# Two edge aggregations of a graph network: waits taken once in four pairs, four gathers on one semaphore

## The reference

```
x = x + _L0_gnn_ref(_layernorm(x), src, dst, edge_weight, W, b)      # layer 1
    msgs = features[edge_src] * edge_weight[:, None]
    agg  = segment_sum(msgs, edge_dst, num_segments=12500)
    out  = einsum('ni,oi->no', agg, W) + b
x = x + _L1_gnn_ref(_layernorm(x), stack([src, dst]), edge_weight, ...) # layer 3
    h = x @ W;  gathered = A_values[:, None] * h[col]
    agg = segment_sum(gathered, row, num_segments=12500)             # then batch norm, relu
```

## Time and profile before

| | before |
|---|---|
| time, median of 3 runs | 8190.22 us |
| span of the profiled execution | 8556.1 us |
| first aggregation, first to last gather | 211.7 to 2484.6 us |
| second aggregation, first to last gather | 4122.7 to 6425.6 us |
| gathers in each / matmul pairs in each | 1563 / 1664 |
| adds of VectorE, both | 3328, 422 ns each |

### The profile page before, as it was taken

One profiled execution on the slowest core, in us unless ns is written; L12 is line 12 of the kernel. 1 busy time (PEld: TensorE's weight loads), 2 busy tenths in 40 slices (PEclk: granted clock), 3 DMA queues, 4 the chain that ended last, 5 costly groups with the idle time before them and its releaser, 6 DMA issues. The chain is left out here.

```text
span 8556.1 us, 91570 instructions
## 1 busy us (share of the span) xinstructions
PE 5764.1 (67%) x19687; PEld 3851.9 (45%) x19687; DVE 4500.6 (53%) x8804; ACT 3777.5 (44%) x9645; POOL 5818.2 (68%) x7545
## 2 busy tenths in 40 slices
PE   5454555555556999968465656565556888888866
PEld 4333333333335666644243434443333555555545
DVE  5354555545456999958454454554457222222227
ACT  5555555655554222226355555555555222222213
POOL 3666666666644222226688888888886688888875
PEclk8677767676665999989666767766678999999988
DMA  7333333333332111126333333333333322222218
GB/s 227 91 90 89 90 91 91 92 91 91 91 116 81 45 50 49 46 65 206 99 90 91 91 89 91 88 91 90 88 91 129 95 59 57 56 58 55 56 47 324
DMA packets 498681, 797.56 MB, mean 93 GB/s; under 512 B 121278, under 2 KB 363563, under 8 KB 498059
## 3 DMA queue, kind: packets, MB, share of 16 engines
q0 software_dynamic: 200256, 453.47, 19.5%
q1 hardware_dynamic: 297904, 338.22, 12.2%
HBM read 595.60 MB, written 197.30 MB: 93 GB/s over the span
## 5 line engine op out<-in xcount | busy, mean ns | idle before, releaser
L1013 PE MATMUL part<-rows,spread 128*128 x6656 | 2481.5, 527 | 1990.5 <-issue 984.0
L1013 PEld LDWEIGHTS part<-rows,spread 128*128 128x128 f32 x6656 | 1613.8, 261 | 2797.6 <-issue 2539.6
L970 DVE TENSOR_TENSOR agg<-agg,part 128x257 f32 (+1 forms) x3328 | 1405.1, 422 | 2230.5 <-PE part L1013 721.7
L953 POOL DMA_INDIRECT rows<-f,row x1563 | 1549.6, 991 | 733.8 <-issue 453.0
L1037 ACT ACTIVATE spread<-iota,place 128x128 f32<-128x128 f32 x3328 | 1016.1, 387 | 2038.2 <-PE part L1013 1309.5
L953 POOL DMA_INDIRECT rows<-h,row x1563 | 1550.5, 992 | 258.4 <-issue 256.3
L1952 POOL DMA_INDIRECT rows<-gat,src x1122 | 1077.9, 961 | 185.0 <-issue 185.0
L1043 ACT ACTIVATE spread<-spread,weight 128x128 f32<-128x128 f32 x3328 | 1017.5, 388 | 14.1 <-ACT spread L1039 0.3
L2030 PE MATMUL y_ps<-agg,hid 128*128 128x256 f32 x3136 | 765.4, 405 | 190.7 <-DVE y_all L2160 190.7
L2030 PEld LDWEIGHTS y_ps<-agg,hid 128*128 128x128 f32 x3136 | 640.9, 206 | 342.2 <-DVE y_all L2160 209.5
L404 POOL COPY spare<-pay 128x1024 f32<-128x1024 f32 x105 | 222.3, 2117 | 735.7 <-DVE pay L391 505.7
(11 more groups left out here) (400 smaller groups left out, 6449.2 us busy)
## 6 DMA issues: line engine op xcount, KB each, us to landing
expert_rows<-y_all SPq DMA_DIRECT2D x196, 256.0 KB
made<-expert_rows SPq DMA_DIRECT2D x49, 1024.0 KB
x<-x SPq DMA_DIRECT2D x42, 896.0 KB
rows<-f,row POOLq DMA_INDIRECT x1563
rows<-h,row POOLq DMA_INDIRECT x1563
rows<-gat,src POOLq DMA_INDIRECT x1122
xbuf<-zero SPq DMA_DIRECT2D x16, 1024.0 KB
x<-xbuf SPq DMA_DIRECT2D x32, 512.0 KB
```

The costliest lines, as they stand in the source:

```text
L953: pool.indirect_dma_start(out=rows[:, u, 0:D], out_offset=None, in_=table, in_offset=bass.IndirectOffsetOnAxis(ap=q.row[:, i:i + 1], axis= ...
L970: nc.vector.tensor_tensor(sum_t, sum_t, part[:, p % NB, 0:WIDE], ALU.add).then_inc(added, 1)
L1013: nc.tensor.matmul(part[:, p % NB, 0:WIDE], spread[:, p % (2 * BANKS), :], row_p, start=True, stop=True).then_inc(multiplied, 1)
```

## The change

It changes who waits how often in `aggregate_edges`; no instruction that computes or moves data is added, removed or reordered. `HAND` is 4.

- The 32 slots share 8 semaphores, four gathers each; SyncE waits for four gathers with one wait and adds four to `landed`: 391 instructions at line 932 for 1563.
- VectorE waits for `multiplied` once in four pairs, for all four; its wait for its own add before stays for every pair.
- TensorE waits for `spread_done` and for free banks once in four pairs, for all four.

```
-        gathered = [s.sem(f"gathered{u}") for u in range(SPAN)]
+        gathered = [s.sem(f"gathered{u}") for u in range(SPAN // HAND)]
...
-                    for i in range(j * BANKS, (j + 1) * BANKS):
+                    for i in range(j * BANKS, (j + 1) * BANKS, HAND):
                         if i < FILLED:
-                            sp.wait_ge(gathered[i % SPAN], i // SPAN * 16 + 16)
-                        sp.sem_inc(landed, 1)
+                            sp.wait_ge(gathered[i % SPAN // HAND], (i // SPAN * HAND + min(HAND, FILLED - i)) * 16)
+                        sp.sem_inc(landed, HAND)
...
-                                            in_offset=bass.IndirectOffsetOnAxis(ap=q.row[:, i:i + 1], axis=0)).then_inc(gathered[u], 16)
+                                            in_offset=bass.IndirectOffsetOnAxis(ap=q.row[:, i:i + 1], axis=0)).then_inc(gathered[u // HAND], 16)
...
                         if u % 4 == 0:
                             tiles = load_tiles(nc, dve, q, p, regs)
-                        dve.wait_ge(multiplied, p + 1)
-
+                            dve.wait_ge(multiplied, p + 4)
                         if p:
                             dve.wait_ge(added, p)
...
-                    pe.wait_ge(spread_done, p + 1)
-                    if p >= NB:
-                        pe.wait_ge(added, p - NB + 1)
+                    if p % 4 == 0:
+                        pe.wait_ge(spread_done, p + 4)
+                        if p + 4 > NB:
+                            pe.wait_ge(added, p + 4 - NB)
```

More of the change, by code:

```diff
@@ L21 @@
 HALF = LANES // 2
-BANKS, RING = 8, 4
+BANKS, RING, HAND = 8, 4, 4
 FILLED = -(-EDGES // P)
```

## The result

| | before | after |
|---|---|---|
| time, median | 8191.28 us (8185.34 to 8197.51, 18 runs) | 8206.51 us (8193.91 to 8228.15, 18 runs) |
| ratio to before | | 1.0020, 95% interval 1.0013 to 1.0026 |
| span of the profiled execution | 8556.1 us | 8203.1 us |

The change makes the kernel 15 us slower. That is little, but the interval of the ratio does not reach 1; 8140 us was forecast. The profiled span, on the other hand, fell by 353 us, to the median. The two do not fit, and the first question is which of the two profiles speaks for the kernel. The profile on which the forecast rests was of a disturbed execution; one further profile would have shown it. From here on, "before" is compared by the first of these new profiles.

What follows compares the result with a forecast made beforehand. GpSimd's gathers were taken to bound both aggregations, with stops at the ring to be won. From the median 8190 us, -44 (stops) and -5 (adds) gave 8141, say 8140 us; the overall range was 8030 to 8210 us.

Steps and rivals of the forecast that it cites:

- What bounds the kernel now: Both aggregations: GpSimd's gathers are the bound, 4576 us, and its 342 us of stops can be won.
- stops at the ring: GpSimd's waits for SyncE's `freed` at line 926 in both aggregations: 342 us profiled, 75 us taken for an ordinary execution.
- rows 4 to 7: Profile rows on SyncE's waits for TensorE, 1109.9 us, adds 0.63 or 2.80 us apart, and long sequencer instructions.
- The part that removes instructions: DVE, PE and SP: 6.7 to 4.5 sequencer instructions a pair, winning 202 us of stops in the profiled execution.
- 59% fewer stops: In slow stretches the chain loses 0.63 us a pair instead of 1.55, so ring stops shrink by about that share.
- What of it is there in an ordinary execution: Both aggregations: unprofiled ring stops are bounded, not known; 75 us taken, gain 44 us, bounds 0 and 202.
- the 44 us of gain: Both aggregations: 59% of the 75 us of ring stops taken for an ordinary execution.
- The first case: If all 366 us are lost in the two aggregations, 83 us are above GpSimd's pace and stops are zero.
- The first rival: Both aggregations: recording makes the slow stretches, GpSimd paces without a stop; no change, 8185 us; chance 0.30.
- The adds themselves: VectorE: three in four adds lose 0.07 us, counting only behind the last gathers, 5 us for both aggregations.
- The other parts: SyncE's shared semaphores, TensorE's matrix and bank waits: up to 3.8 us of lag once, or 0.9 us a group.
- The second rival: Second aggregation, seven banks: TensorE's blocks delay VectorE 1.4 us a group; slower, 8240 us; chance 0.13.

Runs made afterwards that it cites:

- these new profiles: The kernel before, unchanged, profiled twice more: spans 8194.3 and 8190.8 us.
- padded: The changed kernel with each removed wait put back as one already fulfilled: median 8224.22 us, 1.0031 of before.
- step4: The kernel before, each gather keeping its own semaphore, but SyncE counting landed in steps of four: 1.0007 of before.
- pe_dve: The change without SyncE's part, against before: TensorE and VectorE hand over blocks of four, chunks counted one by one: 1.0011 of before.
- before_again: The kernel before, unchanged, profiled again: span 8194.3 us.
- fine_norest_all: Before with TensorE's and VectorE's blocks, pair-by-pair waits in the last 32 pairs, no memsets between second-aggregation and attention gathers: 7768.72 us, 0.9491 of before.

## Why the prediction was wrong

- *What bounds the kernel now.* "GpSimd is the bound" held. "Its stops at the ring are what can be won" did not: in three later profiles of the two kernels there are none. The reading of rows 4 to 7 was a true reading of a disturbed execution. What the chain did in that one execution was taken for what it always does.
- *The part that removes instructions.* 6.7 to 4.5 instructions a pair was right in kind (84,238 for 91,570 in the whole trace), the 59% fewer stops had nothing to act on. The profiled span did fall, by 353 us where 207 were forecast, but not because of the change: unchanged, it fell as far.
- *What of it is there in an ordinary execution.* This is the step that failed. Three values were open for the stops at the ring, 0, 146 and 342 us; 75 us was taken and the measured one is 0, so the 44 us of gain had nothing to come from. The first case had the stops right, but not for its reason, that all 366 us are lost in the aggregations (449 - 366 = 83 us above GpSimd's pace). Before, profiled again, has 83 + 64 = 147 us above the pace, nearly all of them slow gathers: of the 362 us between the two profiles 302 lie between first and last gathers and 34 in the tails. The first rival had the span fall for a reason of its own (the recording), and `padded` and the two profiles of before speak against that reason; its conclusion, that GpSimd paces both aggregations without a stop, is what the runs show.
- *The adds themselves.* 0.07 us off each add was taken: four adds take 2.11 us after, (2.11 - 0.42) / 3 = 0.563 us from one to the next, for 0.63 before, and 0.63 again in `padded`, which has the wait back. The size was right, the place was not. The 60 and 30 adds behind the last gathers were counted from the disturbed profile; before, profiled again, has 16 and 15, worth 31 x 0.75 x 0.07 = 1.6 us instead of 5. And these were not won, since VectorE waits there for TensorE's block. The rule of the Trainium skill ("VectorE: DVE Perf Modes", The DRAIN you can't avoid), that leaving out semaphores between vector operations gains nothing, would have left the adds 0.63 us apart, and that is not what these rows show. The two cases are not alike, though: the wait for the add before stayed here, and what went is a wait instruction of its own that stood between.
- *The other parts.* "Up to 3.8 us of lag, once" was the price of SyncE's steps if their cover was gone. The cover (SyncE waits for TensorE) was gone: it was part of the disturbed execution, and TensorE really waits for SyncE 388 times. The price was met once in each aggregation, +4.8 and +3.3 us (`step4`), and it was not in the sum. Neither was any price for TensorE and VectorE handing over blocks to each other, 9 us (`pe_dve`): this part had looked at each engine's wait by itself.
- *The second rival* had the mechanism and the sign. It expected VectorE to reach its fifth add 3.9 us after the first at the low clock level; 4.59 us were measured. It placed the loss in all groups and took seven banks for its cause, which gave 94 us. Between the gathers it is hidden, and in the tails it shows with eight banks too: 3.5 us there and 5.5 us with seven (`pe_dve`).
- Sum as measured, by the tails: SyncE's steps 8, the blocks 9 us, together 17 of the 18 us by which the tails grew; the medians grew by 15. The forecast had -44 for the stops, -5 for the adds and nothing for the rest. That 17 and 18 agree so well is in part luck, since a tail with blocks varies by some 3 us with the clock, and between the gathers single profiles differ by several us.

## What to carry to other kernels

Before any wait of a profile is read, hold its span against the median of the ordinary runs; here they differed by 4.5% in the one disturbed profile and by at most 0.2% in all others. Where they differ so, take another profile, for the list of waits may be that of another execution. Where one engine paces a long loop, fewer or coarser waits between the others are hidden until its last step, and there they lengthen the tail: coarsen the middle, keep the end fine. And look at what the pacing engine does between its steps, since each 0.1 us there counts once for every step.

## What the runs showed of the hardware

- In one execution (span 8556.1 us) the sequencers of TensorE, VectorE and SyncE needed 0.7 us for register instructions, waits, table loads and asserts alike, one engine after the other: 887 instructions of 0.7 us or more in the first aggregation. The sixteen other profiles of this study show at most seven there, single ones. It is neither the number of recorded instructions nor the kernel: `before_again` has the same 91,570 and none.
- A wait instruction of its own between two vector adds costs 0.07 us, though it is fulfilled and takes 21 ns by its row: the adds stand 0.63 us apart with it (before, `padded`) and 0.563 us without.
- Some of GpSimd's indirect gathers take up to 2.2 us instead of 0.95. In the kernel before, profiled again, that is 157 gathers over 1.05 us in the second aggregation, and 140 of these run beside the sort's step on VectorE, line 386, which reads and writes SBUF alone; 92 others run beside it and are not slow. Of the 2283 gathers of both aggregations beside which VectorE has only adds or nothing, none is slow. In the first aggregation 93 of the 96 slow ones stand beside other lines of the sort (384, 385, 390, 391), and of the 132 gathers beside line 386 none is slow. What makes the difference is not shown. Such gathers make up nearly all that GpSimd needs above its pace. A slow one and its neighbour, from `fine_norest_all`:

```profile
5848.60 1.98 POOL L949 DMA_INDIRECT rows<-h,row  x1 [0.30 <-issue]
5850.88 0.95 POOL L949 DMA_INDIRECT rows<-h,row  x1 [0.30 <-issue]
```
